# A decoder-like chain on one core: the fp4 layer and the output stage become jobs in the attention's slot tables

## The reference

```python
x = x + attn16(layernorm(x)) @ w_proj + b_proj      # 16 heads of 8 channels, dense softmax
x = x + fp4_ffn(layernorm(x))                       # silu(gate) * up, 352 wide, down
x = x + encoder(layernorm(x))                       # 6 layers
x = x + relu(layernorm(x) @ W1 + b1) @ W2 + b2      # 512 wide
```

## Time and profile before

| | us |
|---|---|
| median of 3 runs (lowest, highest) | 2010.36 (2009.47, 2013.61) |
| profiled execution, its own time | 2019.47 |
| span in its trace | 2017.7 |
| TensorE busy | 1660.8 (82%) |
| VectorE busy | 1397.0 (69%) |
| ScalarE busy | 1187.9 (59%) |
| mean granted clock of TensorE | 0.911 |

### The profile page before, as it was taken

How to read it: one execution, slowest core, us unless ns; L and a number is a source line. 1 busy time by engine, 2 the same in 40 slices (tenths; PEclk the granted TensorE clock), 3 DMA queues, 4 the chain that set the end, 5 groups by cost and what they waited for, 6 DMA issues and landing times.

```text
span 2017.7 us, 66915 instructions
## 1 busy us (share of the span) xinstructions
PE 1660.8 (82%) x28905; PEld 921.2 (46%) x28905; DVE 1397.0 (69%) x3285; ACT 1187.9 (59%) x2117; POOL 254.7 (13%) x229
## 2 busy tenths in 40 slices
PE   2889999997564578888888888888889898989677
PEld 1133333332343145555555555555555555555445
DVE  7788888883475665858686867676767675767824
ACT  2057777776312165767666767676766666766542
POOL 1000000000000301212121212120202020202111
PEclk8579999998776589999999999999999899999889
DMA  6022102000002543333333433343243333342001
GB/s 151 16 49 77 37 3 49 2 2 2 14 0 64 117 110 70 88 71 106 85 90 67 114 66 95 66 110 80 71 95 87 96 79 83 70 120 52 5 2 32
DMA packets 152205, 130.83 MB, mean 65 GB/s; under 512 B 65014, under 2 KB 147382, under 8 KB 149894
## 3 DMA queue, kind: packets, MB, share of 16 engines
q1 hardware_dynamic: 134629, 125.75, 25.7%
q10 hardware_dynamic: 17280, 0.79, 0.6%
HBM read 79.25 MB, written 45.88 MB: 62 GB/s over the span
## 4 chain that ended last, share of the span: by engine, by line
PE 54%; DVE 21%; ACT 11%; issue 7%; DMA 6%; POOL 1%; SPq 1%; ACTq 0%; POOLq 0%; DVEq 0%
PE pB L605 12%; PE pO L620 12%; PE pA L590 9%; ACT PB L722 5%; DVE mx L854 5%; PE pG L561 5%; PE pG L571 5%; DMA emr<-sce 3%; PE pG L511 2%; DMA QS<-scq 2%; DVE bst L427 2%; ACT VD L682 2%; ACT HT L637 2%; PE pG L538 1%; PE pG L525 1%
## 5 line engine op out<-in xcount | busy, mean ns | idle before, releaser
L722 ACT ACTIVATE PB<-pB 128x512 f32<-128x512 f32 (+1 forms) x1496 | 836.7, 593 | 478.2 <-PE pB L605 456.8
L854 DVE TENSOR_REDUCE mx<-pA 128x1 f32<-128x512 f32 (+3 forms) x1000 | 636.7, 670 | 146.5 <-PE pA L590 145.5
L605 PE MATMUL pB<-QS,KS 85*32 85x256 bf16 (+3 forms) x11264 | 600.1, 285 | 73.2 <-ACT PB L722 44.5
L590 PE MATMUL pA<-KS,QS 82*32 82x256 bf16 (+2 forms) x8384 | 545.3, 313 | 95.7 <-DMA QS<-scq 48.7
L620 PE MATMUL pO<-PB,VD 128*32 128x128 f32 (+3 forms) x5632 | 459.2, 400 | 5.0 <-issue 3.1
L605 PEld LDWEIGHTS pB<-QS,KS 85*32 85x32 bf16 x11264 | 262.7, 97 | 363.7 <-ACT PB L722 250.9
L590 PEld LDWEIGHTS pA<-KS,QS 82*32 82x32 bf16 x8384 | 203.3, 98 | 319.5 <-DVE mx L854 108.3
L854 DVE TENSOR_REDUCE mxb<-pA 128x1 f32<-128x512 f32 x304 | 207.2, 681 | 9.4 <-PE pA L590 9.4
L450 POOL TENSOR_TENSOR rstd<-vareps,mhalf 128x4 f32<-128x4 f32 x68 | 69.2, 1018 | 1115.7 <-DVE vareps L436 1114.7
L620 PEld LDWEIGHTS pO<-PB,VD 128*32 128x32 f32 x5632 | 160.9, 112 | 32.4 <-issue 5.9
L561 PE MATMUL pG<-HT,wL 128*128 128x512 f32 x192 | 100.4, 650 | 27.4 <-ACT HT L637 25.1
(11 more groups left out here) (160 smaller groups left out, 1517.8 us busy)
## 6 DMA issues: line engine op xcount, KB each, us to landing
scq<-PQ SPq DMA_DIRECT2D x84, 384.0 KB, 3.5
QS<-scq SPq DMA_DIRECT2D x56, 576.0 KB
KS<-sck SPq DMA_DIRECT2D x84, 384.0 KB
sck<-PK SPq DMA_DIRECT2D x28, 384.0 KB, 5.6
wL<-in_wL SPq DMA_DIRECT2D x6, 576.0 KB, 4.9
QS<-mt SPq DMA_DIRECT2D x168, 8.0 KB, 2.1
rE<-in_rE SPq DMA_DIRECT2D x7, 256.0 KB, 12.2
emr<-sce SPq DMA_DIRECT2D x96, 4.0 KB, 1.7
```

The source lines that it names most:

```text
L590: ins = pe.matmul(pA[QT * hd:QT * (hd + 1), a.a_bank(half, n), at:at + width], QS[0:R_A, r // NR, head, r % NR * QT:(r % NR + 1) * QT], ro ...
L605: ins = pe.matmul(pB[32 * i:32 * (i + 1), a.b_bank(h, v), at:at + width], KS[0:R_B, head, k0:k0 + 32], allowed(QS[0:R_B, x, head, :], 3, k ...
L722: act.activation(PB[:, pos_, 0:st.cols], pB[:, a.b_bank(h, v), 0:st.cols], ACT.Exp).then_inc(a.b_exped, 1)
L854: v.tensor_reduce(dst[:, gs[0]:gs[-1] + 1, tl[0]:tl[-1] + 1:step], pA[:, a.a_bank(half, n), 0:len(gs) * len(tl) * st.width] .rearrange("p ...
```

## The change

The fp4 layer is cut by batch and written into the job tables. Jobs beginning with `g` are its pieces: `gl`, `gn`, `gr` (statistics, norm, row quantisation of a chunk, in two parts), `gx` (transposes of a chunk), `gg`, `gs`, `gm` (gate and up, silu, product, per tile), `gq` (quantisation of a unit of two tiles, 704 columns, in two parts), `gh` (transposes of a tile), `gd` (down product and add of a unit), `ge` (encoder input of a batch). Batch 0 runs in the dense table: `gl` to `gr` of both batches where `res` has just been done, the rest in the dense tail, among the last 74 B steps. Batch 1 runs in the sparse table of half 1 at slots -151 to -53, which is the lead-in of the sparse attention (`Half(-1)`, from slot 13) and the first 29 slots of half 0. On ScalarE the silus of batch 0 stand at slots 515, 515, 539, 539, 547, 549, 556, 556 with exponentials between; those of batch 1 at -116 to -66 (relative), all ahead of the first sparse exponential. In that table ScalarE has `gx1` in slot 47 of `Half(-1)`, ahead of `qk00`.

The scratch moves out of `QS`; the weights' quantised copies go to a tile of their own, `wF`, and are transposed before the first dense half (`pe_weights`). Batch 0 has two pairs of banks for gate and up, batch 1 one pair. Loads of the position table, the masks and the first weights move with it.

Jobs beginning with `z` are the output stage, cut by chunk: `za`, `zb`, `zc` on VectorE are `encoder_output`, `zt`, `zh`, `zo` are the last feed-forward on TensorE and ScalarE, `zd` its add. Chunks 0 and 1 run at slots 3 to 49 of the sparse tail, chunks 2 and 3 at slots 43 to 79. The weights of the last feed-forward are loaded into `wF` during the first sparse half. The amount of arithmetic stays as it was.

```diff
         self.jobs = SPARSE_JOBS if sparse else DENSE_JOBS
-        self.end = max(at for t in self.jobs.values() for at, _ in t) - self.period + 1
+        self.end = max(at - (halves - self.owned(name)) * self.period
+                       for t in self.jobs.values() for at, name in t) + 1
...
-                if h is not None:
...
+    def single(self, name):
+
+        return name[0] == "z" or name[0] == "g" and name[1] not in "lnr"
+
+    def owned(self, name):
+
+        if name[0] == "z":
+            return self.halves - B + int(name[2]) // CB
+        if self.single(name):
+            return 1 if self.sparse else 0
+        return self.halves - 1
...
+    "pe": [(-82, "gh5"), (83, "vm0"), (84, "vm1"), (90, "ot0"), (90, "vm2"), (-72, "gd2"), (-151, "gx0"),
+         (97, "vm3"), (-67, "gh6"), (-63, "gh7"), (-59, "gd3"), (106, "ot1"), (188, "zt0"), (108, "ot2"),
+         (190, "zh00"), (191, "zh01"), (191, "zh02"), (191, "zh03"), (192, "zo0"), (111, "aht0"),
+         (194, "zt1"), (113, "wo0"), (195, "zh10"), (195, "zh11"), (195, "zh12"), (119, "ft0"),
+         (119, "hid00"), (119, "hid01"), (119, "hid02"), (119, "hid03"), (120, "ot3"), (120, "out0a"),
+         (120, "out0b"), (202, "zh13"), (121, "aht1"), (125, "wo1"), (-39, "ht0"), (210, "zo1"),
+         (-35, "qk00"), (-34, "qk01"), (-116, "gx1"), (131, "ft1"), (131, "hid10"), (131, "hid11"),
+         (131, "hid12"), (131, "hid13"), (132, "out1a"), (132, "out1b"), (132, "zt2"), (-113, "gg0"),
+         (-31, "v0"), (135, "zh20"), (135, "zh21"), (135, "zh22"), (136, "zh23"), (136, "zo2"),
+         (-27, "ht1"), (-26, "qk10"), (-25, "qk11"), (-104, "gg1"), (-102, "gg2"), (-101, "gg3"),
+         (-99, "gh0"), (148, "zt3"), (-97, "gg4"), (149, "zh30"), (-96, "gh1"), (150, "zh31"),
+         (151, "zh32"), (-94, "gd0"), (-11, "v1"), (-92, "gg5"), (-91, "gh2"), (-90, "gg6"), (156, "zh33"),
+         (-87, "gh3"), (-87, "gg7"), (-86, "gd1"), (161, "zo3"), (-83, "gh4")],
...
+    "dve": [(-80, "gm7"), (-80, "gd1"), (167, "za0"), (86, "vm0"), (-75, "gq30"), (-74, "gq31"), (90, "vm1"),
+          (92, "on0"), (174, "za1"), (175, "zb0"), (-70, "gd2"), (96, "vm2"), (178, "zc0"), (100, "vm3"),
+          (182, "zb1"), (185, "zc1"), (106, "on1"), (108, "on2"), (109, "div0"), (-54, "gd3"), (-53, "ge0"),
+          (193, "zd0"), (113, "res0"), (115, "norm0"), (116, "on3"), (117, "div1"), (-45, "bqs0"),
+          (120, "out0"), (123, "last0"), (124, "res1"), (125, "norm1"), (125, "za2"), (126, "zb2"),
+          (-37, "split00"), (-36, "split01"), (131, "zc2"), (213, "zd1"), (132, "out1"), (-30, "v0"),
+          (134, "last1"), (137, "za3"), (-108, "gm0"), (-25, "split10"), (-25, "split11"), (141, "zb3"),
+          (-104, "gm1"), (142, "zd2"), (-103, "gq00"), (-102, "gm2"), (-101, "gq01"), (-100, "gm3"),
+          (-99, "gq10"), (-98, "gm4"), (-96, "gq11"), (-96, "gm5"), (-95, "gd0"), (-13, "v1"), (151, "zc3"),
+          (153, "zd3"), (-88, "gq20"), (-87, "gm6"), (-87, "gq21")],
...
+    "pe": [(513, "gx0"), (513, "gx1"), (515, "gg0"), (515, "gg1"), (516, "gg2"), (271, "ot2"), (275, "aht0"),
+         (277, "wo0"), (539, "gg3"), (540, "gh0"), (541, "gg4"), (545, "gh1"), (547, "gg5"), (-220, "ht0"),
+         (548, "gd0"), (549, "gh2"), (549, "gg6"), (550, "gh3"), (-216, "ht1"), (557, "gg7"),
+         (-210, "qk00"), (558, "gd1"), (-208, "qk01"), (561, "gh4"), (565, "gh5"), (-200, "qk10"),
+         (569, "gd2"), (-198, "qk11"), (573, "gh6"), (577, "gh7"), (-190, "v0"), (580, "gd3"), (-186, "v1"),
+         (337, "ot3"), (339, "aht1"), (341, "wo1"), (143, "ot0"), (207, "ot1")],
+    "act": [(512, "gx0"), (513, "gx1"), (515, "gs0"), (515, "gs1"), (269, "oev2"), (272, "on2"), (276, "aht0"),
+          (539, "gs2"), (539, "gs3"), (541, "gh0"), (545, "gh1"), (547, "gs4"), (-219, "ht0"), (549, "gs5"),
+          (549, "gh2"), (-215, "ht1"), (553, "gh3"), (556, "gs6"), (556, "gs7"), (-209, "qk00"),
+          (-207, "qk01"), (563, "gh4"), (565, "gh5"), (-199, "qk10"), (-197, "qk11"), (573, "gh6"),
+          (577, "gh7"), (-188, "v0"), (-184, "v1"), (333, "oev3"), (337, "on3"), (340, "aht1"),
+          (141, "oev0"), (144, "on0"), (205, "oev1"), (208, "on1")],
+    "dve": [(512, "gm0"), (518, "gm1"), (521, "gq00"), (522, "gq01"), (273, "div0"), (278, "res0"),
+          (537, "gm2"), (537, "gm3"), (538, "gq10"), (538, "gq11"), (540, "gm4"), (545, "gd0"), (289, "gl0"),
+          (545, "gm5"), (547, "gq20"), (552, "gq21"), (299, "gn0"), (555, "gd1"), (558, "gm6"), (559, "gm7"),
+          (560, "gq30"), (561, "gq31"), (-206, "split00"), (307, "gr00"), (-204, "split01"), (564, "gd2"),
+          (314, "gr01"), (-196, "split10"), (-194, "split11"), (-189, "v0"), (-185, "v1"), (585, "gd3"),
+          (591, "ge0"), (337, "div1"), (340, "res1"), (346, "gl1"), (349, "gn1"), (357, "gr10"),
+          (374, "gr11")],
...
             n = [int(i) for i in name if i.isdigit()]
             kind, x = name.rstrip("0123456789ab"), n[0]
...
             elif kind == "ot":
                 hw(pe, a.o_evac, x + 1, UNITS)
                 pg_free(pe, a, half, name)
+                if not a.sparse and half.off == 1 and x == 2:
+                    pe.wait_ge(gu_done, 2)
...
                     st = a.b[v]
                     x = st.k % 2
+                    if v == 0 and h.off == 0:
+                        if a.sparse:
+                            pe.wait_ge(dn_added, B * FU)
+                        else:
...
+        silu = [[FFw[:, 2 * UW:2 * UW + FF0], x32[:, 1, 0:FF0]],
+                [PBw[:, 4 * CH + FF0 * i:4 * CH + FF0 * (i + 1)] for i in range(2)]]
+        hidt = [ON[:, b * NB:(b + 1) * NB, :, :].rearrange("p t h w -> p (t h w)") for b in range(B)]
...
+        gate_up = [[(pA[:, 0, :], pA[:, 1, :]), (pA[:, 2, :], pG[:, 0, :])], [(pB[:, 0, :], pB[:, 1, :])]]
+        turn = [pG[:, 1, :], pO[:, 0, :]]
...
+                    v.wait_ge(tail_in, 16)
+                v.wait_ge(ln_in, CB * B * LAYERS + c + 1)
+                link_end(v, v.tensor_tensor(n, n, row(rE[:, 0, :]), ALU.mult))
+                link_end(v, v.tensor_tensor(n, n, row(rE[:, 1, :]), ALU.add))
+                ln_stats(v, lnF, N, c)
+            elif kind == "zb":
+                ln_norm(v, lnF, N, N, c)
+                v.wait_ge(lnF.ready, c + 1)
+                link_end(v, v.tensor_tensor(n, n, row(rD[:, 0, :]), ALU.mult))
+                link_end(v, v.tensor_tensor(n, n, row(rD[:, 1, :]), ALU.add))
+                link_end(v, v.tensor_tensor(x, x, n, ALU.add))
+                ln_stats(v, lnD, X, c)
+            elif kind == "zc":
+                ln_norm(v, lnD, X, N, c)
+                v.wait_ge(lnD.ready, c + 1)
+                link_end(v, v.tensor_tensor(x, x, row(rD[:, 2, :]), ALU.add))
+            else:
...
+                if b == 0:
+                    pe.wait_ge(A0.a_reduced, B * A0.na)
...
+            elif kind == "gg":
+                t, pairs = FT * b + n, gate_up[b]
+                pe.wait_ge(f0_ht_ready, CB * (b + 1))
+                if n >= len(pairs):
+                    pe.wait_ge(gu_done, t + 1 - len(pairs))
+                elif b == 0 and n == 1:
+                    pe.wait_ge(A0.ot_read, UNITS + 1)
+                if b == 0 and n == 3:
+                    pe.wait_ge(A0.res, CB + 1)
...
+            elif kind == "gh":
+                u, i = divmod(n, 2)
+                pe.wait_ge(quant, quantised(b, u=u))
+                if b == 0 and n == 0:
+                    pe.wait_ge(A0.aht_ready, CB + 1)
+                if i:
+                    pe.wait_ge(h0_ready, FT * b + n)
+                elif u:
+                    pe.wait_ge(dn_added, FU * b + u)
...
+                    ins = pe.transpose(turn[b][0:WK[k], k * P:(k + 1) * P],
+                                       hid[u % 2][:, i * FF0 + k * P:i * FF0 + k * P + WK[k]], ident[:, :])
+                ins.then_inc(h0_filled, 1)
...
+            elif kind == "gs":
+                t, pairs = FT * b + n, gate_up[b]
+                act.wait_ge(gu_filled, t + 1)
+                if n >= 2:
+                    act.wait_ge(gu_done, t - 1)
+                act.activation(silu[b][n % 2], pairs[n % len(pairs)][0][:, 0:FF0], ACT.Silu).then_inc(gu_silu, 1)
...
+            elif kind == "gq":
+                if part == "0":
...
+                    quantise_scale(v, hid[n % 2], scratch(b, UW))
+                else:
+                    quantise_round(v, hid[n % 2], scratch(b, UW))
+            elif kind == "ge":
+                chunks = range(CB * b, CB * b + CB)
+                v.wait_ge(dn_added, FU * (b + 1))
+                for c in chunks:
+                    ln_stats(v, lnC, X, c)
+                for c in chunks:
+                    ln_norm(v, lnC, X, N, c)
+                v.wait_ge(lnC.ready, lnC.off + CB * (b + 1))
+                v.wait_ge(pos_in, 16)
+                nb = N[:, b * NB:(b + 1) * NB, :]
+                v.tensor_tensor(nb, nb, pos, ALU.add).then_inc(ln_in, CB)
...
```

(68 more changed lines are left out.)

450 lines of the change are left out of this document (193 added, 257 removed), and 35 rows, old and new, of tables (DENSE_JOBS, SPARSE_JOBS).

## The result

The changed kernel takes 1931.6 us (median of 4 runs, 1929.3 to 1932.3) where the kernel before takes 2009.9 (4 runs, 2009.1 to 2013.6): a ratio of 0.9609, 95% interval 0.9593 to 0.9624. The forecast was 1932. Its profiled execution has a span of 1929.7 us and its own time of 1931.5 lies at the median.

A forecast was written before the change was run, and what follows sets the result against it. TensorE was taken to bind the dense loop, and chains of waits the fp4 stage, sparse lead-in and tail. Savings of 57.6 and 21 made 78.6: 2010.4 - 78.6 = 1932 us, itself 1915 to 1950, range 1903 to 1966.

The forecast's parts named there:

- Step 1: Dense half 1: batch 0's rows move in, two chunks partly hidden in VectorE's slack, costing +8 us (between 0 and +16).
- Step 2: Dense tail takes in batch 0's fp4 units: 75 us, between 65 and 90; with step 1, last `res1` 29 later.
- rival 2: Dense tail: waits let the clock fall, half of its 65 us at 1.2 GHz adds 32, giving 1964; chance 0.10.
- Rival 4: Dense tail: each table change also costs a drain, 13.8 us more, giving 1946; chance 0.03.
- Step 3: From last dense `res1` to first sparse B step: 86 us instead of 172.6, 57.6 saved after steps 1 and 2.
- the 14 for the maxima and their merge: Ahead of the first sparse B step: 21 maxima at 0.60 us and their merge take 14 us.
- Rival 1: Better overlap: dense tail at 65 (-10), fp4 batch 1 hidden in the transfer wait, scores at 49 (-13): 1909; chance 0.17.
- the forecast's 20.9 us: Lead-in of the sparse attention: the road through DRAM takes 20.9 us after the splits, so scores could start at 49.
- Step 4: Kernel end: output stage in pieces, -8 us to the end of `out1` and -13 behind it, 21 saved.
- The sum: Whole kernel: 57.6 + 21 = 78.6 us saved, taking the median from 2010.4 to 1932.
- `pe_weights` cost nothing: Before the first dense half: some 5 us of weight transposes and copies lie in a wait; nothing, or +5 without cover.

The follow-up runs named there:

- GpSimd late: GpSimd's products for the first sparse half's residual and sums of V start only after the first sparse B step, against the changed kernel; 1928.4 us (0.9615).
- after again: The changed kernel itself, unedited, run and profiled again in the rounds of the last group; 1932.3 us (0.9621).
- second profile of before: The unchanged kernel before, profiled once more; its span was 2006.0 us.
- the run with `ge0` later: Against the changed kernel, batch 1's input norms moved from slot -53 to -46, behind the first 27 sparse maxima; 1928.9 us (0.9619).
- the kernel with `out1` first: Changed kernel plus GpSimd's late start, later `ge0`, unit 0's earlier fp4 work, and VectorE's last `out1` ahead of `zc2` and `zd1`; 1923.4 us (0.9576).

## Why the prediction was right

**Step 1, the rows in dense half 1: forecast +8.** The last dense transposes of maxima came at 466.3 (456.0 before), and between 464.1 and 470.1 in the other kernels that have the rows there: +8 to +14, on record +10. The step was right within its range.

**Step 2, the dense tail: forecast 75, measured 72.** The clock stayed at 1.00, so rival 2 did not come about. It was worth its place: taken out, the median rose by 21.6 to 25. The working was right in its sums (TensorE 66 forecast, 62 to 63 measured; ScalarE 65 and 60 to 62; VectorE 47 and 45), but its reason for 75 was two engines that hand to each other, and ScalarE's side of it hardly counts: 12.8 us of loads less made the tail 2.5 shorter. TensorE sets the tail: 52.7 us without the units, 19.6 of their 23.0 on top. Behind the tail `res1` took 6.6 us and not 12: `ge0` held `div1` up by 0.4 us at most (its evacuation by ScalarE ended at 540.42, `div1` began at 540.77), so its 5 us were not there. Steps 1 and 2 together put `res1` 23 later instead of 29.

**Table loads.** 58 against 48, ten more, and each 1.283 us. ScalarE's timeline in the dense tail after:

```profile
468.88 1.28 ACT L1305 ACT_TABLE_LOAD   x1
470.17 0.46 ACT L1305 ACTIVATE FF<-pA 128x352 f32<-128x352 f32 x1
471.31 0.46 ACT L1305 ACTIVATE x<-pA 128x352 f32<-128x352 f32 x1 [0.67 <-PE pG L1267]
471.79 1.28 ACT L795 ACT_TABLE_LOAD   x1
473.08 2.19 ACT L795 ACTIVATE PB<-pB 128x512 f32<-128x512 f32 x4
```

A silu follows 0.01 us after its load and an exponential 0.01 us after its own: no drain is seen. Rival 4 was wrong, and by the run without silu even the 12.8 us cost no more than 2.5.

**Step 3, from `res1` to the first B step: forecast 86, measured 94.3.** Splits done at 30.3 (28 forecast), first maximum at 64.4 (scores effectively at 62), merge done 17.8 later (14), `ge0` 9.8 (7). Three terms were too small. The norms beside GpSimd are two: the rows of the last chunk, put at 9.7, and `ge0`, put at 7, each took some 3 us more than undisturbed. The third is the 14 for the maxima and their merge. It left out that the fourth unit's transposes and down product still stand between the scores on TensorE: VectorE waits 0.31 and 2.34 us for them among the maxima and does two adds of 0.41, so 17.8, and with GpSimd late too. That the run without GpSimd's work then shows 87.4, close to 86, is in part luck: there the first maximum came at 61.0 and not at 62, and the last piece took 8.6 and not 10. The price was in the trace of before and was read over: VectorE's norms of a batch took 5.49 us at 658.2, beside the same work of GpSimd. Since this miss (8 us late) and that of steps 1 and 2 (6 early) are opposite, the first B step came 55.2 sooner where 57.6 was forecast. Rival 1's transfer was no limit: by the forecast's 20.9 us the data could have been there at 51, but VectorE has only 3.2 us of waits from the last split to the first maximum.

**Step 4, the end: forecast 21, measured 17.7 to 18.0.** To the products of `out1` -6.1 where -8 was forecast, and here two errors cancel in part. The block and its wait brought 7.8, not 11.8, with a rest of about 1. The feed-forward put in cost 0.8, not some 4, because it fills waits and because it keeps the clock up (0.80 before; 1.00 after, 0.95 in after again), a term that the forecast put at nothing. Behind the products -11.6 where -13 was forecast.

**The sum.** 78.6 forecast and 78.3 measured between the medians on record, 76.3 between after's span and the second profile of before: 55.0 + 18.0 and 3.3 from the untouched halves, which the forecast put at nothing. They lie ahead of the first division of half 0, which comes 86.4 us behind the first B step before and 82.1 after; the rest of the stretch takes 1100.4 and 1101.4. It fits what the run with `ge0` later shows, that time lost just ahead of the first B step is in part given back there, but no run tests it by itself. The agreement to 0.4 us is luck; the terms missed by 6, 8 and 3 us. `pe_weights` cost nothing: the first dense maximum came at 57.58 and 57.30.

## What to carry to other kernels

Work of a waiting stage that is put into a busy pipeline costs about what the engine that sets its pace serialises there, not what the stage takes alone: batch 0's units, 38.3 us standing alone, added 19.6 to the dense tail, and held TensorE for 23.0. Work that fills an engine's waits can also keep its clock up and shorten what stands around it. When a stage's start is pulled forward, look from which event the following waits count: here B steps 9 us sooner brought 4, because what they wait for dates from the scores. And where a kernel's executions differ by more than an edit is worth, compare landmarks of traces, stretch by stretch, before believing a median, and set a median only beside one of the same rounds.

## What the runs showed of the hardware

VectorE and GpSimd disturb each other. Four fp32 norms (`TENSOR_SCALAR`, SBUF to SBUF, two columns as scalars) took 1.11 us alone and 4.25 beside GpSimd; seven reductions from PSUM took 4.27 us at 637.2 in after, beside the same products of GpSimd, and 4.34 at 612.4 without them. A `TENSOR_TENSOR` with two inputs in SBUF took 1.64 instead of 0.69 at the end of the kernel, next to a product of GpSimd that also grew, from 1.26 to 1.64:

```profile
1885.48 0.68 DVE L1208 TENSOR_TENSOR N<-N,rE 128x512 f32<-128x512 f32 x1
...
1886.19 1.64 DVE L1209 TENSOR_TENSOR N<-N,rE 128x512 f32<-128x512 f32 x1
...
1885.64 1.64 POOL L952 TENSOR_TENSOR HB<-N,rL 128x512 f32<-128x512 f32 x1 [1.23 <-DVE N L490]
```

The Trainium skill (SBUF — State Buffer, "SBUF: two separate sides") describes this as one pair of ports that the two engines take in turn, each for a whole instruction, with VectorE concerned when it runs in a two-port mode, or when it reads two tensors of SBUF and GpSimd's instruction reads SBUF too, as these do. By that rule the product with two inputs is slowed and the reductions, which read PSUM, are free, and the trace agrees; for the norms it agrees if they run in a two-port mode, which no run here shows by itself.

The length of a sparse half goes with its granted clock. In 117 halves of thirteen profiles (the second to the tenth of each), those with a clock of 1.00 took 101.3 to 104.1 us, mean 102.4 (19 halves); 0.98, 103.2 (46); 0.97, 105.0 (37); 0.95, 104.8 to 107.9, mean 106.2 (15). The first of each, left out here, spread more: the two longest, 109.2 and 109.0, had 0.95 too. The DMA share does not go with the length (correlation -0.15, the clock's -0.81). Two halves in a row of one execution, the windows of the kernel with `out1` first:

```profile
1023.90:1131.10 107.20, 93.06 (x1940) 60.05 (x1936) 73.91 (x191) 70.71 (x125) 18.71 (x16) 0.95 0.37 90
1131.10:1233.00 101.90, 89.11 (x1944) 57.63 (x1936) 73.37 (x192) 70.80 (x125) 19.51 (x18) 1.00 0.34 82
```

The same instructions, 5.3 us apart. The clock goes with a part of what spreads the executions of one kernel, not with all of it: the two profiles of before differ by 5.5 us over ten halves (1043.5 and 1038.0) at mean clocks of 0.976 and 0.977, so the 9 us by which the one on record exceeded its median have no cause shown. Whether the clock falls first and lengthens the half, or a late hand-over lets the clock fall, was not tried.
